# Small products on column groups of TensorE, norms eight units apart, and a new order of the beginning, in one transformer block on one core

## The reference, cut to what matters

```python
mod = (silu(c) @ wmod).reshape(16, 6, 1, -1)          # sa, ca, ga, sb, cb, gb
h = layernorm(x) * (1 + ca) + sa
beta = softplus(h @ b_w.T + b_b)                      # 16 heads
q, k, v = (h @ w.T + bias for each)                   # 16 heads of 128
out = ((l2norm(q) @ l2norm(k).T) * mask) @ (beta * v) # in chunks of 64
x = x + ga * ((out * silu(h @ og_w.T)) @ o_w.T + o_b)
h = layernorm(x) * (1 + cb) + sb
scores = softmax(h @ gate_w.T)                        # 16 experts, top 6
x = x + gb * (sum of weighted experts(h) + shared(h))
```

## Time and profile before

| | |
|---|---|
| median of 3 runs | 2196.67 us (2196.66 to 2197.76) |
| the profiled execution | 2196.34 us |
| its span | 2194.6 us |
| mean granted clock of TensorE | 0.996 |
| busy: PE, DVE, ACT, POOL | 2157.6, 1168.7, 1030.2, 537.1 us |

### The profile page before, as it was taken

One profiled execution on the slowest core, in us unless ns is written; L12 is line 12 of the kernel. 1 busy time (PEld: TensorE's weight loads), 2 busy tenths in 40 slices (PEclk: granted clock), 3 DMA queues, 4 the chain that ended last, 5 costly groups with the idle time before them and its releaser, 6 DMA issues.

```text
span 2194.6 us, 36065 instructions
## 1 busy us (share of the span) xinstructions
PE 2157.6 (98%) x12444; PEld 1784.9 (81%) x12444; DVE 1168.7 (53%) x2171; ACT 1030.2 (47%) x3284; POOL 537.1 (24%) x540
## 2 busy tenths in 40 slices
PE   7999999999999999999999999999999999999999
PEld 6777888888888888888888887888888888888887
DVE  4455556555556555555555454555555455545554
ACT  4555555555565655555655453333333332323332
POOL 2334334344334334334344342000000000000000
PEclk8999999999999999999999999999999999999999
DMA  7464462453543643542433130352334234323221
GB/s 238 166 205 155 161 164 55 146 165 84 153 145 93 175 149 89 164 145 74 144 117 97 39 135 15 125 188 96 121 106 168 92 115 143 113 100 120 88 100 63
DMA packets 191892, 274.79 MB, mean 125 GB/s; under 512 B 99184, under 2 KB 132960, under 8 KB 191712
## 3 DMA queue, kind: packets, MB, share of 16 engines
q1 hardware_dynamic: 191712, 272.49, 39.4%
HBM read 214.79 MB, written 57.67 MB: 124 GB/s over the span
## 4 chain that ended last, share of the span: by engine, by line
PE 81%; DVE 1%; ACT 1%; issue 1%; DVEq 0%; ACTq 0%
PE proj_ps L641 43%; PE out_ps L641 13%; PE av_ps L852 4%; PE s_ps L897 3%; PE av_ps L897 3%; PE kt_ps L897 3%; PE qt_ps L897 3%; PE s_ps L841 3%; PE qt_ps L822 2%; PE kt_ps L827 2%; PE misc_ps L669 1%; PE out_ps L707 0%; ACT squares L1065 0%; PE misc_ps L660 0%; DVE gated L1377 0%
## 5 line engine op out<-in xcount | busy, mean ns | idle before, releaser
L641 PE MATMUL proj_ps<-w_qkv,h_t 128*128 128x512 f32 x2304 | 617.5, 406 | 14.7 <-DVE q_sb L1356 8.1
L641 PEld LDWEIGHTS proj_ps<-w_qkv,h_t 128*128 128x128 f32 x2304 | 409.6, 188 | 105.2 <-issue 15.1
L641 PE MATMUL proj_ps<-h_t,w_qkv 128*128 128x512 f32 x1800 | 443.8, 391 | 0.0
L641 PEld LDWEIGHTS proj_ps<-h_t,w_qkv 128*128 128x128 f32 x1800 | 335.9, 188 | 69.0
L598 POOL TENSOR_TENSOR inv_norm<-guarded,minus_half 128x8 f32<-128x8 f32 x128 | 209.5, 1637 | 647.5 <-DVE guarded L1369 647.4
L1056 ACT ACTIVATE q_t<-qt_ps 128x512 f32<-128x512 f32 x128 | 76.3, 596 | 314.7 <-PE qt_ps L822 314.7
L641 PE MATMUL proj_ps<-h_t,w_gate 128*128 128x512 f32 x768 | 185.4, 396 | 0.6 <-PE misc_ps L695 0.3
L1356 DVE TENSOR_TENSOR q_sb<-proj_ps,bias 128x512 f32<-128x512 f32 x128 | 88.0, 687 | 180.1 <-PE proj_ps L641 173.3
L1065 ACT ACTIVATE squares<-q_sb 128x128 f32<-128x128 f32 x512 | 151.4, 298 | 67.9 <-DVE q_sb L1356 63.9
L641 PEld LDWEIGHTS proj_ps<-h_t,w_gate 128*128 128x128 f32 x768 | 141.9, 189 | 31.7 <-ACT gate L1079 2.3
L1356 DVE TENSOR_TENSOR v_sb<-proj_ps,bias 128x512 f32<-128x512 f32 x128 | 88.5, 691 | 145.6 <-PE av_ps L852 145.1
(11 more groups left out here) (202 smaller groups left out, 3225.5 us busy)
## 6 DMA issues: line engine op xcount, KB each, us to landing
w_qkv<-tile_scr SPq DMA_DIRECT2D x100, 768.0 KB, 4.3
w_qkv<-head_scr SPq DMA_DIRECT2D x45, 1024.0 KB, 11.6
head_scr<-stage SPq DMA_DIRECT2D x30, 512.0 KB, 3.2
w_gate<-head_scr SPq DMA_DIRECT2D x15, 1024.0 KB, 4.9
w_out<-head_scr SPq DMA_DIRECT2D x15, 1024.0 KB, 5.3
tile_scr<-stage SPq DMA_DIRECT2D x25, 512.0 KB, 3.3
x_in<-_attn_hidden_states_dram SPq DMA_DIRECT2D x16, 512.0 KB, 7.6
h_scr<-stage SPq DMA_DIRECT2D x16, 512.0 KB, 3.3
```

The costliest lines, as they stand in the source:

```text
L641: mm = pe.matmul(out, w, y, start=(j == 0 and m == 0), stop=(3 * j + m == n - 1))
```

## The change

- `beta` and `logits` swap their operands. The 16 columns of `b_w` and the 16 of `gate_w` lie side by side in `small_wt` (128x32) and are the stationary operand; 128 columns of `h_f` move. The four tiles `t` write to four groups of 32 output partitions of one bank. ACT copies the 128x128 result to `small`, and new tasks `zturn` and `lturn` turn it back with one transpose on PE. The DVE work of `beta` and `logits` moves to the new tasks.
- `mod_product` does the same with `silu_t` (doubled to 32 columns); ACT copies (`copy_mod`), and `mod_turn` turns with one and two transposes.
- In `plan()` the two first norms of a quarter stand 8 units apart, at units 15 and 23 of each 32 in place of 18 and 22; `stats` to `split` and `exp` to `sum` each take a place of their own. `prep` and `tile` keep out of second places that hold `exp`, `log` or `prob`. `prep` may start at any unit after 1 and ends up to one unit later: V of group 1 is staged in unit 6 (before: units 4 and 5), G in unit 7 (before: 6), O in unit 8 (before: 7).
- `prefetch` is called for each place, after its stores.
- The beginning: Q's weights are issued ahead of `wmod`. PE: Q's boot chunks, `mod_product(0)`, one half of the turn, `mod_turn`, the other half, then K's and V's chunks and `beta`. DVE takes the second half of the modulation from ACT. `exp` and `one` of supertile 0 move from ahead of unit 0 and its first place to its second place, after the squares; `log`, `soft`, `sum` and the stats of supertile 1 move to unit 1, where V's bias goes ahead of `sum_squares`. `mod_product(1)` stands between O's two boot chunks, `mod_turn` after them.

```diff
@@ plan @@
-    put(0, 0, "one", 0)
-    put(0, 0, "log", 0)
-    put(0, 1, "soft", 0)
-    put(0, 1, "sum", 0)
-    first_norm(1, (0, 1), (1, 0), (2, 0), (2, 1), (3, 0), (3, 0), (3, 1), (4, 0), (4, 1), (5, 0), (5, 1))
+    put(0, 0, "zturn", 0)
+    put(0, 1, "exp", 0)
+    put(0, 1, "one", 0)
+    for step in ("log", "soft", "sum"):
+        put(1, 0, step, 0)
+    first_norm(1, (1, 0), (1, 1), (2, 0), (2, 1), (3, 0), (3, 0), (3, 1), (4, 0), (4, 1), (5, 0), (5, 1), (5, 1))
...
-            n = 32 * q + 18 + 4 * a
-            first_norm(2 * (q + 1) + a, *((n + u, p) for u, p in ((0, 0), (1, 0), (1, 1), (2, 0), (2, 1), (2, 1), (4, 0),
-                                                                  (4, 1), (5, 0), (5, 1), (6, 1))))
-    free = lambda n, p: (n % TS, p) != (1, 1) and not any(t[0] in CHUNKS or t[:2] == ("split", "f") for t in side[n, p])
+            n = 32 * q + 15 + 8 * a
+            first_norm(2 * (q + 1) + a, *((n + u, p) for u, p in ((0, 0), (0, 1), (1, 0), (1, 1), (2, 0), (2, 1), (3, 0),
+                                                                  (3, 1), (4, 0), (4, 1), (5, 0), (5, 1))))
+    free = lambda n, p: (n % TS, p) != (1, 1) and not any(t[0] in CHUNKS + p * ("prob", "exp", "log") or t[:2] == ("split", "f") for t in side[n, p])
@@ sync @@
-                            load_weights(gi + 1, kind)
+                        if n == max(prep_end[g, kind] + 1, 8 * g - 2 if kind == G else 0):
+                            load_weights(g, kind)
...
                     for task in side[n, p]:
                         stores(task)
-                prefetch(n)
+                    prefetch((n, p))
@@ tensor @@
-                    for t in range(TS):
-                        for h in range(KC):
-                            mm = pe.matmul(misc[:, t * NH:(t + 1) * NH], h_f[:, h, t * P:(t + 1) * P], w[:, h, :],
-                                           start=(h == 0), stop=(h == KC - 1))
+                    for h in range(KC):
+                        for t in range(TS):
+                            mm = pe.matmul(misc[t * (NH + E):(t + 1) * (NH + E), 0:P], small_wt[:, h, :],
+                                           h_f[:, h, t * P:(t + 1) * P], start=(h == 0), stop=(h == KC - 1))
...
+                elif kind == "zturn" or kind == "lturn":
+                    misc = chunk(task)
+                    pe.wait_ge(small_copied, small_at[small_of(task)] + 1)
+                    if task == ("zturn", 0):
+                        pe.wait_ge(boot_lo, 5)
+                    pe.transpose(misc[:, 0:P], small[:, 0, :], ident).then_inc(side_filled, 1)
...
+                for i, piece in enumerate(pieces):
                     for h in range(KC):
-                        mm = pe.matmul(ps[:, w * B:(w + 1) * B], pieces[w // 4][h][:, (w % 4) * P:(w % 4 + 1) * P],
-                                       silu_t[:, h, :], start=(h == 0), stop=(h == KC - 1))
+                        for r in range(4):
+                            mm = pe.matmul(ps[r * 2 * B:(r + 1) * 2 * B, i * P:(i + 1) * P],
+                                           silu_t[:, h, :, :].rearrange("p a b -> p (a b)"),
+                                           piece[h][:, r * P:(r + 1) * P], start=(h == 0), stop=(h == KC - 1))
...
             for h in range(KC):
-                do(("turn", "a", 0, h))
-            for kind in (Q, K):
-                for h in range(KC):
-                    boot_chunk(kind, h)
+                boot_chunk(Q, h)
+            mod_product(0, proj_ps[1], [raw[Q]])
+            do(("turn", "a", 0, 0))
+            mod_turn(0, proj_ps[0], 1)
+            do(("turn", "a", 0, 1))
+            for h in range(KC):
+                boot_chunk(K, h)
@@ scalar @@
+                elif kind == "beta" or kind == "logits":
+                    j = small_at[task]
+                    act.wait_ge(side_filled, chunk_at[task] + 1)
...
+                    act.activation(small[:, 0, :], misc[:, 0:P], ACT.Copy).then_inc(small_copied, 1)
```

More of the change, by code:

```diff
@@ L39 @@
 Q, K, V, G, O = range(5)
-CHUNKS = ("turn", "beta", "x1", "logits", "wturn", "prep", "tile", "final")
+CHUNKS = ("turn", "beta", "zturn", "x1", "logits", "lturn", "wturn", "prep", "tile", "final")
 NI = NQ * NG * 2
@@ L77, in first_norm @@
         for at, task in zip(places, (("stats", "a", s), ("norm", "a", s), ("turn", "a", s, 0), ("turn", "a", s, 1),
-                                     ("split", "a", s), ("beta", s), ("exp", s), ("one", s), ("log", s), ("soft", s),
+                                     ("beta", s), ("split", "a", s), ("zturn", s), ("exp", s), ("one", s), ("log", s), ("soft", s),
                                      ("sum", s))):
@@ L289, in build @@
         norm_at = {t[1:3]: j for j, t in enumerate(t for t in order if t[0] == "norm")}
+        small_order = [t for t in order if t[0] in ("beta", "logits")]
+        small_at = {t: j for j, t in enumerate(small_order)}
+        turn_of = lambda t: ({"beta": "zturn", "logits": "lturn"}[t[0]], t[1])
+        small_of = lambda t: ({"zturn": "beta", "lturn": "logits"}[t[0]], t[1])
         staged = []
@@ L472, in _, with prefetch @@
                 if v and ("norm", kind, s) in last_use:
-                    coming.setdefault(last_use.get(("norm", *norms[v - 1]), -1), []).insert(0, ("x", kind, s))
-            def prefetch(n):
-                for t in coming.get(n, ()):
+                    coming.setdefault(last_use.get(("norm", *norms[v - 1])), []).insert(0, ("x", kind, s))
+            def prefetch(place):
+                for t in coming.get(place, ()):
                     if t[0] == "x":
@@ L922, in _ @@
                 if n < 2:
-                    for h in range(KC):
-                        boot_chunk((G, O)[n], h)
+                    boot_chunk((G, O)[n], 0)
                 if n == 1:
-                    pe.wait_ge(boot_lo, 9)
-                    mod_product(1, s_ps, late_wmod)
+                    pe.wait_ge(boot_lo, 7)
+                    mod_product(1, s_ps[:, 0:2 * P], late_wmod)
+                if n < 2:
+                    boot_chunk((G, O)[n], 1)
+                if n == 1:
+                    mod_turn(1, s_ps[:, 2 * P:4 * P], 2)
                 if n < N:
@@ L1040, in boot_part, with copy_mod @@
                 act.activation(to, boot_ps[j][:, :], ACT.Copy).then_inc(boot_hi, 1)
+            def copy_mod(j, ps, n):
+                act.wait_ge(mod_ready, j + 1)
+                if j:
+                    act.wait_ge(side_filled, chunk_at["zturn", 0] + 1)
+                act.activation(small[:, 0:n, :].rearrange("p a n -> p (a n)"), ps[:, 0:n * P], ACT.Copy)\
+                   .then_inc(mod_copied, 1)
+            boot_part(Q, 0)
+            boot_part(Q, 1)
+            copy_mod(0, proj_ps[1], 1)
             do(("turn", "a", 0, 0))
-            do(("turn", "a", 0, 1))
-            boot_part(Q, 0)
-            do(("split", "a", 0))
-            boot_part(Q, 1)
+            for h in range(KC):
+                act.wait_ge(modulated, h + 1)
+                m = act.activation(h_t[:, 0, h, 0, :], h_f[:, h, :], ACT.Copy)
+            m.then_inc(h_hi_done, 1)
             boot_part(K, 0)
@@ L1050, in _ @@
             boot_part(V, 1)
-            do(("exp", 0))
+            do(("beta", 0))
             def copy_turned(n):
@@ L1115, in _ @@
                     hi_part(n - 1)
+                if n == 1:
+                    copy_mod(1, s_ps, 2)
                 if n < 2:
@@ L1186, in do @@
                                               ALU.subtract).then_inc(stage_lo, 1)
-                elif kind == "beta":
+                elif kind == "zturn":
                     s = task[1]
@@ L1315, in _ @@
             boot_part(Q, 0)
+            boot_part(Q, 1)
+            turned = ("turn", "a", 0, 1)
+            dve.wait_ge(side_filled, chunk_at[turned] + 1)
+            dve.wait_ge(gained, 2)
+            dve.wait_ge(modulated, 1)
+            for j in range(BS):
+                m = dve.tensor_scalar(h_f[:, 1, j * L:(j + 1) * L], side_bank[turned][0][:, j * L:(j + 1) * L],
+                                      mod[:, CA * KC + 1, j:j + 1], mod[:, SA * KC + 1, j:j + 1], ALU.mult, ALU.add)
+            m.then_inc(modulated, 1)
+            dve.wait_ge(modulated, 2)
+            dve.nop().then_inc(side_bank[turned][1], 1)
             do(("split", "a", 0))
-            boot_part(Q, 1)
             boot_part(K, 0)
```

100 lines of the change are left out of this document (58 added, 42 removed).

## The result

The changed kernel takes **2176.03 us** (median of 4 runs, 2175.14 to 2177.27) against 2196.66 for the kernel before: a ratio of 0.9906, 95% interval 0.9889 to 0.9923. The forecast was 2166, with a range of 2158 to 2178. Of the 30.4 us that the sum promised, 20.6 came.

What follows compares the result with a forecast made beforehand. PE was taken as the bound, busy 2157.6 of 2194.6 us. Terms 12.9 + 12 + 3.8 + 1.0 + 2.2 - 1.5 = 30.4 us off 2196.34 gave 2165.9, with the median's 0.33 some 2166; range 2158 to 2178.

Steps and rivals of the forecast that it cites:

- Small products: Beta and logits blocks in the steady part: four column groups at once save 0.86 us a block, 12.9 us for 15.
- The beginning: Start of the run up to the first gate projection: gate at 33.2 instead of 46.42; 12 us taken, bounds 6 and 15.
- The waits of units 2 to 127: PE's waits after the beginning: 3.8 us around unit 4, 1.0 behind split and beta, 2.2 for o_w would go.
- The 2.2 us for `o_w`: PE's wait for O's weights goes because loads are issued by place, half a unit earlier; 2.2 us, bounds 0 and 2.2.
- The 1.0 us for `split` and `beta`: Waits for Q's bias in units after a second place with both tasks shrink; 1.0 us, bounds 0 and 1.8.
- What is added: V's weights of group 1, staged one unit later, may land late for unit 8; loss of 1.5 us, bounds 0 and 5.
- Two groups at once: Rival: in the changed small-product blocks only two column groups overlap, cutting the gain; 2174 us, chance 0.18.
- one group at a time: Rival: the changed small-product blocks get no overlap between column groups, 19.8 us less than forecast; 2186 us, chance 0.05.
- a clock that falls behind the blocks: Rival: after each grouped block PE's clock drops, 3.4 us a stretch, 51 us for 15; 2217 us, chance 0.04.
- The beginning gave all: Answers a rival that the beginning gives half, through loads or ACT's longer chain; 6 us less, 2172 us, chance 0.17.
- time freed on PE that turns into waits: Rival: nothing comes of the change because PE then waits for DVE or ACT; within 0.2% (4.4 us), chance 0.03.
- signs of being wrong: Starts in twos, new waits at units 1 and 8, low clock behind blocks, or span shrinking less than PE's busy time.

Runs made afterwards that it cites:

- experiment 4: Changed kernel with the loops of beta and logits exchanged, so a tile's four instructions follow each other on one column group; 2177.83 us.
- experiment 7: Changed kernel with loads of prep weights, tile weights and x issued once both places of a unit are stored, as before the change; 2178.25 us.
- experiment 1: Changed kernel with stats and norm of supertiles 2 to 7 one place earlier, so a place lies between norm and turn; 2169.2 us.
- experiment 2: As experiment 1, with split ahead of beta, beta in its unit's second place and zturn a place later (supertiles 2 to 7); 2164.56 us.

## Why the prediction was right, and where it was off

- *Small products, 12.9 us forecast.* The mechanism, four groups at once, was right, and so was the reading of the earlier trace rows. The size is close: 1.04 us less for a block in its place and 0.11 for the turn, so 0.93 against 0.86, 14.1 us for the 15 (with 1.10 for the block behind a wait). Two errors of the term partly cancel. The old block takes 1.70 us of the stream, not the 1.86 of its busy time, and the new one 0.66, not 0.89: I had given it the whole 0.89 us around the score block, edges of its neighbours included. The Trainium skill, "TensorE: Matmul & The Clock Gate", on packing small matmuls, has products start and end in program order. The trace here doesn't agree: with a group's four instructions in a row the starts still come four at a time and the block takes 0.67 us (experiment 4).
- *The beginning, 12 us forecast with 13.2 worked out.* 13.9 measured at the first gate. The walk held step by step: first projection 17.0 (16.9 said), first squares 19.9 (20.0), V of unit 1 at 26.46 (26.1), squares of unit 1 from 28.2 (28.3), gate at 32.51 (33.2). The clock stayed high, so the deduction for it was not needed, and the gate itself gained: from its start to the next projection it is 5.55 us in place of 6.60, 1.05 more for the beginning.
- *The waits of units 2 to 127, 3.8 + 1.0 + 2.2 forecast.* Between the starts of the first two gates the gain is 6.8 us. Less 1.05 for the gate's clock, 1.21 for one block and some 0.3 for one `prep` less and one turn more, 4.3 are the waits of units 4 and 5 and the low clock, 3.8 said. The reading of these waits was off in one point: the 0.30 us stood at 74.92, ahead of `log`, whose tables load from 79.97 on. It belongs to the `exp` and `prep` of unit 3. The 2.2 us for `o_w` came, though for which reason is open (experiment 7). The 1.0 us for `split` and `beta` came where it was looked for and was lost elsewhere: the two waits behind these places, 0.73 and 0.82 us, are gone, and waits for Q's bias of 0.47 and 0.96 us at 109.63 and 154.30 are new. With the 0.9 in the beginning Q's bias still holds PE 2.3 us.
- *What is added, 1.5 us forecast.* **This is the step that failed.** I looked at the weights of group 1, which cost 0.5 us (a wait at 101.08), and costed the new places of norm, turn and beta only as cover for DVE. I never asked how long PE needs from one place to the next: `norm` in a second place and `turn` in the next first place leave DVE 0.7 us for a norm of 2.17, and `beta` in the place behind the turn's second half leaves ACT too little for `h_f`. That cost 6.8 + 4.6 = 11.4 us by experiments 1 and 2; some 3 us of it (0.79 in each of three norms, 0.72 in a fourth) is the norm's greater length beside POOL's work, which the forecast did not look at either.
- *The balance.* 14.1 + 13.9 + 1.05 + 4.3 + 2.2 - 0.5 - 11.4 = 23.7 us against 20.6 measured. About 3 us are not assigned; experiment 2, which has not lost the 11.4, is 31.6 us below the kernel before and so 3.5 short of the 35.1 that it should have. The terms of this sum come from different traces and runs, each with an interval of some 3 us.
- *The rivals.* Two groups at once, one group at a time and a clock that falls behind the blocks are excluded: all 16 blocks are at 0.65 us, and from 14.56 to 2100 us PEclk is 1.00 but for the one stretch behind a wait for x. The beginning gave all. What took the gain was on no list: the nearest, time freed on PE that turns into waits, I had dismissed by the busy shares of DVE and ACT.
- *The range.* That 2176 lies in it is in part luck. Its high end, 2178, was set by two groups at once together with part of the beginning lost, and neither happened; a loss that the forecast did not know filled the same room. By the number alone the rival with two groups at once (2174) fits better than the forecast (2166).
- *The signs.* Right came the block at 0.65 us with starts in fours, the gate at 32.5 and no wait for `nat`. Of the signs of being wrong two showed: the span shrank by less than PE's busy time (19.8 against 22.9 us), and V's weights of group 1 were waited for. PEclk was not 1.00 throughout from 40 us on.

## What to carry to other kernels

When a task is moved to another place of a hand-written order, cost the distance in the consumer's time, not only the cover for the producer: here PE asked for x 0.7 us after DVE had begun a norm of 2.17. A busy share of 53% says nothing about that. Look also at what the other engines do at the new place, since the same norm takes 1.38 us elsewhere. These small products with one short side were worth turning round onto column groups even with a copy and a transpose behind them (0.93 us a block). And where PE waited for its own result only to raise a semaphore, it stood still some 0.4 us each time; letting the others wait for the first semaphore's count took 10.2 us off in 40 places.

## What the runs showed of the hardware that was not expected

- Products on four column groups start four at a time even where the program has all four instructions of one group in a row (experiment 4), and the block is the same 0.65 to 0.67 us.
- Of the 64 norm instructions (128x256, one of four for a supertile) 60 take 0.40 to 0.41 us. The other four take 1.13 to 1.20, one in each of the norms at 186.23, 271.71, 595.90 and 925.86, and each runs beside POOL's scaling of Q (line 606, 1.04 to 1.06 us) for nearly all of that operation; no other norm instruction lies beside it for more than 0.2 us. Beside POOL's inverse norm (line 603, at 513.02 and 842.94) they keep their 0.41. In experiment 1, where POOL does nothing during a norm, all 16 norms take 1.38 us. A run with POOL's work alone moved was not made.
- After the 2.4 us wait for x near 598 us the clock was at 1.2 GHz for 3.4 us; after those at 188, 274 (1.6 us each) and 928 (2.1 us) it stayed at 2.4 GHz. The same wait of 2.4 us near 600 us in experiment 7 left it at 2.4 GHz, and there it fell behind the wait of 2.1 us at 929.
